# Scaling expert results as they leave PSUM, and accumulating them into x by DMA

## The chip, the cores and the metric

One core of a Trainium2 chip runs the whole program in one launch. The metric is the time of one execution on the device, in microseconds (us). The engines are TensorE (PE, with its weight loads as PEld), VectorE (DVE), ScalarE (ACT), GpSimd (POOL) and SyncE (SP, which only issues DMAs here). POOL issues the indirect DMAs, those whose row numbers come from a tile of indices.

## The reference, cut to what matters

Four steps update x, which has 4 x 512 tokens of 512 numbers. The change touches the second and the seam to the third.

```python
x = x + gat(ctx_512, layernorm(x))           # L0 xattn, two graph attention layers
x = x + moe(layernorm(x))                    # L0 ffn: 8 experts, each token goes to 2
x = x + image_attention(layernorm(x), ctx)   # L1 xattn
x = x + sparse_ffn(layernorm(x))             # L1 ffn, 2:4 sparsity in the hidden layer

# L0 ffn
router_logits = x_flat @ gate_w.T
top_w, sel = top_k(router_logits, 2)
top_w = softmax(top_w)
tw = zeros((n, E)).at[tok_ids, sel].add(top_w)
h  = silu(g) * u                             # g, u: gate and up products of each expert
eo = einsum('enf,edf->end', h, down_proj)
out = einsum('end,ne->nd', eo, tw)           # each token: two expert rows, each by its weight
```

## The kernel before, in words

x lives in SBUF as `X`, 16 tiles of 128 tokens x 512. The program is a row of blocks (`nc.Block`), each with one hand-written instruction stream per engine; semaphores order the streams, and an engine works strictly in the order of its own stream. Every f32 product is three matmuls on a high and a low part (`product3`, lines 72 to 74).

`route` computes, for every token, its two slots among REAL = 39 blocks of 128 slots (`rt["slot"]`, 128 x 32 indices), the two weights (`rt["weight"]`), and the list of tokens of each block. To make that list DVE builds one-hot tiles `blk_hot` (128 x 32 x 39) and `off_hot` (128 x 32 x 128), and PE multiplies them (line 1113).

`moe` runs the 39 blocks of slots. POOL gathers a block's token rows (`m_rows`), PE turns them (line 1402), ACT and DVE split the result, PE forms gate and up, then down into one of two PSUM banks `ACC`; ACT copies that to `y` (`result`, line 1473), and SP stores `y` in the DRAM scratch `y_dram`. The rows stored are not yet scaled.

`image_attention` starts with POOL fetching the rows of y for chunk 0 (4 tiles, 2 rows a token: 8 indirect DMAs into `pair`) and, after the norm of chunk 0, those of chunk 1. Meanwhile the keys are made by PE, ACT and DVE. DVE adds the pairs of chunks 0 and 1, scaled, to X (`add_pairs`, line 1799). For chunks 2 and 3 ACT scales them (`scale_pair`, line 1746) and POOL adds them (`add_pair`, line 1650). Each chunk then goes through: DVE statistics (line 119); POOL 1/sqrt (`pool_rstd_for_act`, lines 132 and 134); ACT normalizes (line 141); PE turns; ACT and DVE split; PE forms o and then the similarities; DVE centres and scales them (lines 1827 to 1846), ACT takes exp (line 1753) and DVE adds to X (line 1851). The norm of chunk b + 1 stands inside the work on chunk b, at i = 0 of the loop over i, and needs chunk b + 1 complete in X. POOL also makes one small number a tile (`rs_of`, line 1659), in line with its DMAs. `ffn` follows.

What sets the order around the change is thus each engine's hand-written stream. The functions are below.

Of the kernel before, what the change touches and what calls it, by code (L numbers as in the profile page):

```python
# [15 lines left out]
BF16 = mybir.dt.bfloat16  # L16
# [970 lines left out]
def route(nc, outer, dram):  # L987
# [8 lines left out]
    with ExitStack() as ctx:  # L996
# [41 lines left out]
        lane_b = sb("lane_b", [P, 1], BF16)  # L1038
        off_hot = sb("off_hot", [P, J, P], BF16)
        blk_hot = sb("blk_hot", [P, J, REAL], BF16)  # L1040
        blk_tok = sb("blk_tok", [P, J, 2, REAL], BF16)
# [222 lines left out]
def moe(nc, outer, dram):  # L1264
# [10 lines left out]
    with ExitStack() as ctx:  # L1275
# [11 lines left out]
        hT_lo = sb("hT_lo", [P, 2, RE, P], F32R)  # L1287
        y = sb("y", [P, 2, D])

        GATE = [ps[:, 0, 0:FE], ps[:, 1, 0:FE]]  # L1290
# [12 lines left out]
        gu_lo, dn_lo = sem("m_gu_lo"), sem("m_dn_lo")  # L1303
        index_ready = sem("m_index_ready")
        gu_hi, dn_hi, ld_gu, ld_dn = rt["gu_hi"], rt["dn_hi"], rt["ld_gu"], rt["ld_dn"]

# [24 lines left out]
        with nc.Block() as block:  # L1331
# [66 lines left out]
            def _(pe):  # L1398
# [31 lines left out]
                def body(g, j, i):  # L1430
# [20 lines left out]
                turn_rows(1, 1)  # L1451
                pipeline(pe, body)
                turn_hidden(REAL - 1, 0)
# [3 lines left out]
            def _(act):  # L1457
# [39 lines left out]
                rows_hi(1, 1)  # L1497
                split(1, slice(1, 2), range(DC))
                pipeline(act, body)
                hidden_hi(REAL - 1, 0)  # L1500
# [6 lines left out]
            def _(dve):  # L1507
# [40 lines left out]
                dve.memset(hid[:, :, :], 0.0).then_inc(hid_made, 2)  # L1548
                dve.wait_ge(hid_made, 2)
                dve.sem_inc(gu_lo, 1)  # L1550
                rows_lo(0, 0)
                hidden(0, 0)
# [11 lines left out]
def image_attention(nc, outer, dram):  # L1564
# [7 lines left out]
    with ExitStack() as ctx:  # L1572
        def sb(name, shape, dt=F32):
            return ctx.enter_context(nc.sbuf_tensor("a_" + name, shape, dt))

        pair = [sb(f"pair{k}", [P, D]) for k in range(2 * TB)]
        x_hi = sb("x_hi", [P, 2, DC, N], F32R)
# [36 lines left out]
        dve_chain = sem("a_dve_chain")  # L1614
        paired = [sem(f"a_paired{k}") for k in range(2 * TB)]
        added, scaled, summed = sem("a_added"), sem("a_scaled"), sem("a_summed")

        with nc.Block() as block:
            @block.sync
            def _(sp):  # L1620
                sp.dma_start(gamma[:, :], dram["gamma"].broadcast_to([P, N])).then_inc(ld_row, 16)
                sp.dma_start(beta[:, :], dram["beta"].broadcast_to([P, N])).then_inc(ld_row, 16)

                sp.wait_ge(added, 4 * TB)
                for r in range(2):
                    sp.dma_start(outer["raw_gu"][:, r, :, :], dram["ffn_gu"][r]).then_inc(outer["ld_gu"][r], 16)
                for r in range(RQ):
                    sp.dma_start(outer["raw_dn"][:, r, :], dram["ffn_dn"][r]).then_inc(outer["ld_dn"][r], 16)

            @block.gpsimd  # L1630
            def _(pool):
                def gather(c, i):

                    for k in range(2):
                        if c in (1, 2):
                            pool.wait_ge(added, TB * (2 * c - 2 + k) + i + 1)
                        if c == 3:
                            pool.wait_ge(summed, 2 * i + k + 1)
                        j = 2 * (TB * c + i) + k
                        pool.indirect_dma_start(out=pair[2 * i + k][:, :], out_offset=None, in_=rt["y_dram"],  # L1640
                                                in_offset=bass.IndirectOffsetOnAxis(ap=rt["slot"][:, j:j + 1], axis=0)
                                                ).then_inc(paired[2 * i + k], 16)

                def add_pair(c, i):
                    t, n = TB * c + i, 2 * (TB * (c - 2) + i)
                    for k in range(2):
                        pool.wait_ge(scaled, n + k + 1)
                        if k == 1:
                            pool.wait_ge(summed, n + 1)
                        pool.tensor_tensor(X[:, t, :], X[:, t, :], pair[2 * i + k][:, :], ALU.add).then_inc(summed, 1)  # L1650

                for i in range(TB):
                    gather(0, i)
                norm.pool_rstd_for_act(pool, 0)
                for i in range(TB):
                    gather(1, i)
                def rs_of(t):
# [70 lines left out]
            def _(act):  # L1728
# [12 lines left out]

                def scale_pair(c, i):
                    for k in range(2):
                        t, pk = TB * c + i, pair[2 * i + k]
                        act.wait_ge(paired[2 * i + k], 16 * (c + 1))
                        act.activation(pk[:, :], pk[:, :], ACT.Identity,
                                       scale=rt["weight"][:, t, k:k + 1]).then_inc(scaled, 1)

                def exp_of(t):
# [19 lines left out]
                for b in range(B):  # L1769
                    for i in range(TB):  # L1770
# [3 lines left out]
                        if b + 1 < B and i % 2 == 0:  # L1774
# [7 lines left out]
                        if b + 2 < B and i >= 1:  # L1782
                            scale_pair(b + 2, i - 1)
                    if b + 1 < B:
                        o_hi_of(b + 1)
                    if b + 2 < B:
                        scale_pair(b + 2, TB - 1)

            @block.vector
            def _(dve):  # L1790
                chain = Chain(dve, dve_chain)
                def add_pairs(c, k):

                    for i in range(TB):
                        t = TB * c + i
                        dve.wait_ge(paired[2 * i + k], 16 * (c + 1))
                        if k == 1:
                            dve.wait_ge(added, 2 * TB * c + i + 1)
                        dve.scalar_tensor_tensor(out=X[:, t, :], in0=pair[2 * i + k][:, :],
                                                 scalar=rt["weight"][:, t, k:k + 1], in1=X[:, t, :],  # L1800
                                                 op0=ALU.mult, op1=ALU.add).then_inc(added, 1)
                    dve.wait_ge(added, TB * (2 * c + k + 1))

                def x_lo_of(c, i):
# [3 lines left out]
                for b in range(B):  # L1808
# [4 lines left out]
                    dve.tensor_scalar(kvT[:, :], KVB, bk[:, 0:1], None, ALU.add).then_inc(kvT_made, 1)  # L1813
                    if b >= 2:
                        add_pairs(0, b - 2)
                    dve.wait_ge(kvT_hi_done, b + 1)
# [31 lines left out]
                def add_prob(t):  # L1848
# [3 lines left out]
                                             in1=X[:, t, :], op0=ALU.mult, op1=ALU.add).then_inc(x_added, 1)  # L1852

                norm.dve_stats_for_act(chain, 0)
                dve.wait_ge(ld_row, 32)
# [5 lines left out]

                add_pairs(1, 0)
# [253 lines left out]
def build(nc, dram, out):  # L2116
    with ExitStack() as ctx:
# [39 lines left out]
        with ExitStack() as kv_inputs, ExitStack() as experts:  # L2157
# [6 lines left out]
            for name, shape in (("gu_w", [P, 2, DC, 2, FE]), ("dn_w", [P, 2, RE, D])):  # L2164
                for part in ("_hi", "_lo"):
                    route_[name + part] = experts.enter_context(nc.sbuf_tensor(name + part, shape, F32R))
            route(nc, outer, dram)
            moe(nc, outer, dram)
# [65 lines left out]
```

## Time and profile before

| | |
|---|---|
| times of three runs | 1205.3, 1206.35, 1206.38 us; median 1206.35 |
| profiled execution | 1207.65 us, of which the span of the profile is 1205.9 |
| busy share | PE 81%, PEld 67%, DVE 56%, ACT 30%, POOL 23% |
| route ends, moe starts | 198.3 us from the span's start |
| moe ends, attention starts | 484.4 us |
| attention's last DVE operation ends | 646.29 us |

A profile row of the timeline gives the start, the duration, the engine, the line in the kernel, the operation, what it writes and reads, and in brackets how long the engine had been idle and which event ended that. For POOL, DMA_INDIRECT is the time in which POOL writes the transfer's descriptors; the data moves afterwards. PEclk is the TensorE clock that was granted: 1.00 is 2.4 GHz, 0.50 is 1.2 GHz.

### The profile page before, as it was taken

Reading aid. Unit: us, or ns where it says so; the run is one execution under the profiler, and the core shown is the slowest. Engines: PE = TensorE matmul, PEld = TensorE weight load, DVE = VectorE, ACT = ScalarE, POOL = GpSimd, SP = SyncE. Lnnn points to the kernel's source line nnn. Section 1 sums busy time; section 2 is a strip of 40 time slices with the busy share of each in tenths; the row PEclk is TensorE's granted clock in tenths of the full one; section 3 lists DMA queues with packets and bytes.
Section 4 is the critical chain, followed back from the end, with each engine's and each line's share of the span. In section 5 each row is a group of like instructions: output and inputs, shape, how many; then the busy total and the mean of one; then the engine's idle time right before and its main releaser. Section 6 shows DMA issues by size and latency. Waiting matters only on the chain. (4 is left out here: it accounts for less than half of the span.)

```text
span 1205.9 us, 15539 instructions
## 1 busy us (share of the span) xinstructions
PE 972.1 (81%) x4555; PEld 806.1 (67%) x4556; DVE 673.8 (56%) x1391; ACT 363.4 (30%) x608; POOL 283.1 (23%) x297
## 2 busy tenths in 40 slices
PE   4980711999999998433356789999999999999996
PEld 3760311899999997222245678888888888888885
DVE  6963775343243522576788754554556555454545
ACT  4760310342243433223333321322132212212220
POOL 0574131223123510446613200301011100301000
PEclk8995765999999999576667989999999999999998
DMA  8165303444244421341201100201001100100001
GB/s 335 45 143 95 131 9 136 146 144 170 70 144 152 161 78 44 105 157 42 63 1 48 58 1 2 70 1 35 0 35 35 35 0 0 35 0 1 35 35 70
DMA packets 35833, 86.32 MB, mean 72 GB/s; under 512 B 5840, under 2 KB 5968, under 8 KB 34512
## 3 DMA queue, kind: packets, MB, share of 16 engines
q1 hardware_dynamic: 27216, 62.76, 14.8%
q0 software_dynamic: 8576, 23.08, 7.2%
q8 instruction: 18, 0.29, 0.1%
q14 instruction: 23, 0.19, 0.1%
HBM read 63.01 MB, written 22.81 MB: 71 GB/s over the span
## 5 line engine op out<-in xcount | busy, mean ns | idle before, releaser
L72 PE MATMUL ps<-f_x_lo,f_w_hi 128*128 128x512 f32 x512 | 202.9, 396 | 14.1 <-POOL f_w_lo L919 7.3
L73 PE MATMUL ps<-f_x_hi,f_w_lo 128*128 128x512 f32 x512 | 201.8, 394 | 0.0
L74 PE MATMUL ps<-f_x_hi,f_w_hi 128*128 128x512 f32 x512 | 201.6, 394 | 0.0
L981 DVE TENSOR_TENSOR f_hid<-f_sg,ps 128x512 f32<-128x512 f32 x64 | 43.7, 684 | 196.7 <-ACT f_sg L976 196.5
L72 PEld LDWEIGHTS ps<-f_x_lo,f_w_hi 128*128 128x128 f32 x512 | 97.6, 191 | 35.8 <-DVE f_hid L981 7.2
L74 PEld LDWEIGHTS ps<-f_x_hi,f_w_hi 128*128 128x128 f32 x512 | 97.7, 191 | 20.7
L73 PEld LDWEIGHTS ps<-f_x_hi,f_w_lo 128*128 128x128 f32 x512 | 97.7, 191 | 20.4
L72 PE MATMUL ps<-gu_w_lo,m_xT_hi 128*128 (+1 forms) x312 | 105.8, 339 | 3.1 <-DVE m_xT_lo L1510 3.1
L976 ACT ACTIVATE f_sg<-ps 128x512 f32<-128x512 f32 x64 | 38.2, 599 | 227.4 <-PE ps L74 227.1
L72 PE MATMUL ps<-f_w_lo,kv_c_hi 128*128 128x512 f32 x256 | 102.1, 399 | 5.4 <-DVE x L2102 5.4
L73 PE MATMUL ps<-f_w_hi,kv_c_lo 128*128 128x512 f32 x256 | 102.0, 398 | 0.0
L74 PE MATMUL ps<-f_w_hi,kv_c_hi 128*128 128x512 f32 x256 | 101.8, 398 | 0.0
L74 PE MATMUL ps<-gu_w_hi,m_xT_hi 128*128 (+1 forms) x312 | 101.4, 325 | 0.0
L73 PE MATMUL ps<-gu_w_hi,m_xT_lo 128*128 (+1 forms) x312 | 101.3, 325 | 0.0
L919 POOL TENSOR_TENSOR f_w_lo<-raw,f_w_hi 128x1024 fp32r<-128x1024 f32 x16 | 38.5, 2406 | 252.9 <-ACT f_w_hi L909 252.9
L1520 DVE TENSOR_TENSOR m_hT_lo<-ps,m_hT_hi 128x384 fp32r<-128x384 f32 x39 | 21.7, 555 | 115.2 <-ACT m_hT_hi L1464 97.2
L2001 ACT CAST kv_c_hi<-f_hid 128x1024 fp32r<-128x1024 f32 x32 | 33.6, 1050 | 149.7 <-PE ps L74 117.7
L2067 DVE TENSOR_TENSOR f_beats<-kv_c_raw 128x768 bf16<-128x768 f32 (+2 forms) x96 | 65.7, 739 | 22.7 <-ACT kv_c_raw L1995 18.8
L159 PE MATMUL ps<-ident,a_a_xn 128*128 128x128 f32 x64 | 15.7, 427 | 65.7 <-ACT a_a_xn L141 64.3
L72 PEld LDWEIGHTS ps<-gu_w_lo,m_xT_hi 128*128 128x128 f32 x312 | 59.2, 190 | 8.9 <-issue 4.9
L72 PEld LDWEIGHTS ps<-f_w_lo,kv_c_hi 128*128 128x128 f32 x256 | 48.6, 190 | 17.3 <-DVE kv_c_lo L2096 5.8
L73 PEld LDWEIGHTS ps<-gu_w_hi,m_xT_lo 128*128 128x128 f32 x312 | 59.3, 190 | 0.5
(301 smaller groups left out, 1930.6 us busy)
## 6 DMA issues: line engine op xcount, KB each, us to landing
raw<-in_moe_gu SPq DMA_DIRECT2D x32, 352.0 KB
y_scratch<-m_y SPq DMA_DIRECT2D x39, 256.0 KB
raw<-in_ffn_gu SPq DMA_DIRECT2D x16, 512.0 KB, 3.5
raw<-in_moe_dn SPq DMA_DIRECT2D x24, 256.0 KB
x<-in_x SPq DMA_DIRECT2D x4, 1024.0 KB, 13.3
gat_rows<-g_ybuf SPq DMA_DIRECT2D x16, 256.0 KB
xn_scratch<-r_r_xn SPq DMA_DIRECT2D x16, 256.0 KB, 2.2
raw<-in_ffn_dn SPq DMA_DIRECT2D x16, 256.0 KB
```

The lines of the kernel that those rows point to most:

```text
L72: eng.matmul(out, lhs_hi, rhs_lo, start=start, stop=False)
L73: eng.matmul(out, lhs_lo, rhs_hi, start=False, stop=False)
L74: return eng.matmul(out, lhs_hi, rhs_hi, start=False, stop=stop)
L159: ins = eng.transpose(bank[:, P * d:P * d + P], self.xn[:, t % self.nb, P * d:P * d + P], self.ident[:, :])
L919: pool.tensor_tensor(self.w_lo[r][:, 0:2, :], self.raw_gu[:, r % self.slots, :, :], self.w_hi[r][:, 0:2, :].bitcast(F32), ALU.subtract).th ...
L976: act.activation(sg[:, k, :], self.GATE[k], ACT.Silu).then_inc(self.silu, 1)
L981: dve.tensor_tensor(out, sg[:, k, :], self.UP[k], ALU.mult).then_inc(self.hid_made, 1)
L1520: dve.tensor_tensor(hT_lo[:, k, :, :], HB.rearrange("p (r n) -> p r n", r=RE), hT_hi[:, k, :, :].bitcast(F32), ALU.subtract).then_inc(h_lo ...
L2001: act.copy(hid_hi[:, 0, :, half], hid[:, :, half]).then_inc(u.hid_hi_done, 1)
L2067: ins = dve.tensor_tensor(beats[:, at:at + n, :], mag[:, i, half].unsqueeze(1).broadcast_to([P, n, HN]), mag[:, j0:j1, half], ALU.is_ge)
```

## The change

Each slot's weight is now brought into slot order. At the start of `moe` DVE writes the weights as a sum of three bf16 terms (five small operations), multiplies `blk_hot` by each term (three operations of 128 x 1248), PE multiplies by `off_hot` in 32 matmuls of 117 columns into `ACC[1]`, and DVE adds the three parts to `slot_weight` (128 x 39). `result` becomes an activation Identity with that scale. For this `off_hot` and `blk_hot` live on after `route`. In `image_attention` the tiles `pair`, `add_pairs`, `scale_pair` and `add_pair` go; POOL fetches the rows with accumulating indirect DMAs straight into X, first all k = 0 of a chunk and then all k = 1, and DVE waits on `second_in` before it takes a chunk's statistics.

```diff
+                pe.wait_ge(weight_hot, 1)
+                for j in range(2 * T):
+                    ins = pe.matmul(ACC[1][:, 0:3 * REAL], off_hot[:, j, :],
+                                    blk_weight[:, j, :, :].rearrange("p w b -> p (w b)"), start=(j == 0),
+                                    stop=(j == 2 * T - 1))
+                ins.then_inc(weight_sum, 1)
                 turn_rows(0, 1)
...
-                    act.copy(y[:, k, :], ACC[k]).then_inc(y_done, 1)
+                    at = slice(g, g + 1) if isinstance(g, int) else bass.ds(g, 1)
+                    act.activation(y[:, k, :], ACC[k], ACT.Identity, scale=slot_weight[:, at]).then_inc(y_done, 1)
...
+                for n in range(3):
+                    ins = dve.tensor_tensor(blk_weight[:, :, n, :], blk_hot[:, :, :],
+                                            weight_b[:, n, :].unsqueeze(2).broadcast_to([P, 2 * T, REAL]), ALU.mult)
+                ins.then_inc(weight_hot, 1)
...
-                sp.wait_ge(added, 4 * TB)
+                sp.wait_ge(second_in[1], 16 * TB)
...
+                def fetch(c, k, tiles):
+
+                    for i in tiles:
+                        t = TB * c + i
                         if k == 1:
+                            pool.wait_ge(first_in[i], 16 * (c + 1))
+                        pool.indirect_dma_start(out=X[:, t, :], out_offset=None, in_=rt["y_dram"],
+                                                in_offset=bass.IndirectOffsetOnAxis(
+                                                    ap=rt["slot"][:, 2 * t + k:2 * t + k + 1], axis=0),
+                                                compute_op=ALU.add).then_inc((first_in[i], second_in[c])[k], 16)
+
+                for k in range(2):
+                    fetch(0, k, range(TB))
+                for k in range(2):
+                    fetch(1, k, range(TB))
                 norm.pool_rstd_for_act(pool, 0)
-                for i in range(TB):
-                    gather(1, i)
...
-                            gather(b + 2, i)
-                            if i >= 1:
-                                add_pair(b + 2, i - 1)
-                    if b + 2 < B:
-                        add_pair(b + 2, TB - 1)
+                            fetch(b + 2, i // 2, range(TB // 2 * (i % 2), TB // 2 * (i % 2) + 2))
...
-                    if b == 0:
-                        add_pairs(1, 1)
-                    else:
-                        dve.wait_ge(summed, 2 * TB * b)
+                    dve.wait_ge(second_in[b + 1], 16 * TB)
```

POOL's stream at the start of the attention block, before: line 1640 is a fetch, lines 132 and 134 are the norm, 1659 is `rs_of`, 1650 an addition to x.

```order
L1640 DMA a_pair<-y_scratch,slot 128x512 x8
L132 TENSOR_TENSOR a_a_rstd<-a_a_var_eps,minus_half 128x4
L134 TENSOR_TENSOR a_a_minus_mean<-a_a_minus_mean,a_a_rstd 128x4
L1640 DMA a_pair<-y_scratch,slot 128x512 x8
L1659 TENSOR_TENSOR a_rs<-a_ve,minus_half 128x1 x2
L132 TENSOR_TENSOR a_a_rstd<-a_a_var_eps,minus_half 128x4
L134 TENSOR_TENSOR a_a_minus_mean<-a_a_minus_mean,a_a_rstd 128x4
L1640 DMA a_pair<-y_scratch,slot 128x512 x2
```

The same place in the changed kernel, where line 1680 is the accumulating fetch and 1692 is `rs_of`:

```order
L1680 DMA x<-y_scratch,slot 128x512 x16
L132 TENSOR_TENSOR a_a_rstd<-a_a_var_eps,minus_half 128x4
L134 TENSOR_TENSOR a_a_minus_mean<-a_a_minus_mean,a_a_rstd 128x4
L1692 TENSOR_TENSOR a_rs<-a_ve,minus_half 128x1 x2
L132 TENSOR_TENSOR a_a_rstd<-a_a_var_eps,minus_half 128x4
L134 TENSOR_TENSOR a_a_minus_mean<-a_a_minus_mean,a_a_rstd 128x4
L1680 DMA x<-y_scratch,slot 128x512 x2
```

The eight fetches of chunk 1 stood behind the first norm and now stand ahead of it.

DVE's stream at the start of `moe`, in the changed kernel; before, line 1525's operation came straight behind the memset:

```order
L1563 MEMSET m_hid 128x768
L1566 CAST m_weight_b<-weight 128x32
L1568 TENSOR_TENSOR m_weight_rest<-weight,m_weight_b 128x32
L1570 CAST m_weight_b<-m_weight_rest 128x32
L1572 TENSOR_TENSOR m_weight_rest<-m_weight_rest,m_weight_b 128x32
L1574 CAST m_weight_b<-m_weight_rest 128x32
L1577 TENSOR_TENSOR m_blk_weight<-blk_hot,m_weight_b 128x32x39 x3
L1584 COPY m_slot_weight<-ps 128x39
L1586 TENSOR_TENSOR m_slot_weight<-m_slot_weight,ps 128x39
L1589 TENSOR_TENSOR m_slot_weight<-m_slot_weight,ps 128x39
L1525 TENSOR_TENSOR m_xT_lo<-ps,m_xT_hi 128x512
```

Eleven small or middle-sized operations have come in between the memset and the split of the first rows; PE's 32 matmuls wait for the first nine of them.

## Rows read from the trace of the kernel before

**Rows 1.** Windows: the ffn, then three stretches within moe.

```profile
core 0: us, PE busy (x) PEld busy (x) DVE busy (x) ACT busy (x) POOL busy (x), PEclk, DMA share, GB/s
637.20:1205.90 568.70, 543.20 (x2352) 443.14 (x2352) 319.44 (x700) 136.20 (x178) 61.60 (x35) 0.98 0.08 26
208.63:211.73 3.10, 3.10 (x10) 3.10 (x11) 0.00 (x0) 0.53 (x1) 0.00 (x0) 0.50 1.02 402
211.96:213.72 1.76, 1.76 (x12) 1.76 (x12) 0.00 (x0) 0.47 (x1) 0.00 (x0) 1.00 0.07 28
216.30:474.00 257.70, 257.67 (x1519) 238.06 (x1519) 94.18 (x148) 93.52 (x178) 73.56 (x115) 1.00 0.37 126
```

**Rows 2.** Timeline of DVE and PE, end of route and start of moe.

```profile
183.34 0.18 DVE L1224 TENSOR_SCALAR r_at<-slot 128x32 int32<-128x32 int32 x1
186.74 1.45 DVE L1233 TENSOR_TENSOR r_blk_tok<-r_blk_hot,r_lane_b 128x1248 bf16<-128x1248 bf16 x1
192.58 2.26 PE L1113 MATMUL ps<-r_blk_tok,r_off_hot 128*128 128x78 bf16 x32 [17.64 <-DVE r_off_hot L1235]
198.74 0.70 DVE L1548 MEMSET m_hid<- 128x768 f32 x1 [0.79 <-DVEq L1055]
206.12 1.11 PE L1402 MATMUL ps<-ident,m_rows 128*128 128x128 f32 x4 [11.27 <-DMA m_rows<-xn_scratch,m_index]
```

**Rows 3.** Groups of ACT, whole span.

```profile
L1473 ACT COPY m_y<-ps 128x512 f32<-128x512 f32 x39 | 22.9, 587 | 54.1 <-PE ps L74 51.0 <-issue 3.0
L1746 ACT ACTIVATE a_pair<-a_pair,weight 128x512 f32<-128x512 f32 x16 | 11.1, 715 | 16.2 <-DMA a_pair<-y_scratch,slot 16.2
```

**Rows 4.** Timeline of POOL, start of the attention.

```profile
485.14 0.94 POOL L1640 DMA_INDIRECT a_pair<-y_scratch,slot  x1 [37.98 <-POOLq L1331]
487.64 1.43 POOL L1640 DMA_INDIRECT a_pair<-y_scratch,slot  x1 [0.30 <-issue]
506.62 1.05 POOL L132 TENSOR_TENSOR a_a_rstd<-a_a_var_eps,minus_half 128x4 f32<-128x4 f32 x1 [11.12 <-DVE a_a_var_eps L126]
```

**Rows 5.** Tiles: issue (ns, min/median/max) of accumulating fetches; landing of plain ones (a_pair).

```profile
L337 POOL DMA_INDIRECT x<-gat_rows,g_arg x16: 1539/1548/1597, 63.3 to 103.7; - x16
DMA to landing us min/median/max: 3.4/3.5/3.9
```

**Rows 6.** Timeline and windows, plain and accumulating fetches of the first stage.

```profile
74.61 0.94 POOL L315 DMA_INDIRECT g_arg<-gat_arg,g_place  x1 [0.31 <-issue]
103.67 1.55 POOL L337 DMA_INDIRECT x<-gat_rows,g_arg  x1 [0.30 <-issue]
...
107.00:109.00 2.00, 0.00 (x0) 0.00 (x0) 0.00 (x0) 0.00 (x0) 0.00 (x0) 0.50 0.59 101
109.00:110.00 1.00, 0.00 (x0) 0.00 (x0) 0.00 (x0) 0.00 (x0) 0.00 (x0) 0.50 0.03 4
```

**Rows 7.** Timeline of DVE in the attention.

```profile
487.56 0.69 DVE L1817 TENSOR_TENSOR a_kvT_lo<-a_kvT,a_kvT_hi 128x512 fp32r<-128x512 f32 x1 [0.69 <-ACT a_kvT_hi L1731]
503.39 2.46 DVE L119 BATCH_NORM_STATS2 a_a_stats<-x 128x6 f32<-128x512 f32 x4
527.43 2.73 DVE L1799 SCALAR_TENSOR_TENSOR x<-a_pair,weight,x 128x512 f32<-128x512 f32 x4
540.59 1.44 DVE L1843 SCALAR_TENSOR_TENSOR kv_c_raw<-kv_c_raw,a_rs,a_beta 128x512 f32<-128x512 f32 x1
575.76 1.51 DVE L1843 SCALAR_TENSOR_TENSOR kv_c_raw<-kv_c_raw,a_rs,a_beta 128x512 f32<-128x512 f32 x1
613.07 0.74 DVE L1843 SCALAR_TENSOR_TENSOR kv_c_raw<-kv_c_raw,a_rs,a_beta 128x512 f32<-128x512 f32 x1
```

**Rows 8.** Timeline of POOL and DVE, chunk 2 becoming complete.

```profile
556.80 0.55 POOL L1659 TENSOR_TENSOR a_rs<-a_ve,minus_half 128x1 f32<-128x1 f32 x1 [5.62 <-DVE a_ve L1830]
558.84 0.95 POOL L1640 DMA_INDIRECT a_pair<-y_scratch,slot  x1 [0.30 <-issue]
565.43 2.47 DVE L119 BATCH_NORM_STATS2 a_a_stats<-x 128x6 f32<-128x512 f32 x4 [3.78 <-POOL x L1650]
```

More of the change, by code:

```diff
@@ L1288, in moe @@
         y = sb("y", [P, 2, D])
+        off_hot, blk_hot = rt["off_hot"], rt["blk_hot"]
+        weight_b = sb("weight_b", [P, 3, 2 * T], BF16)
+        rest = sb("weight_rest", [P, 2 * T])
+        blk_weight = sb("blk_weight", [P, 2 * T, 3, REAL], BF16)
+        slot_weight = sb("slot_weight", [P, REAL])
         GATE = [ps[:, 0, 0:FE], ps[:, 1, 0:FE]]
@@ L1304, in moe @@
         index_ready = sem("m_index_ready")
+        terms, weight_hot, weight_sum, weight_made = (
+            sem("m_" + n) for n in ("terms", "weight_hot", "weight_sum", "weight_made"))
         gu_hi, dn_hi, ld_gu, ld_dn = rt["gu_hi"], rt["dn_hi"], rt["ld_gu"], rt["ld_dn"]
@@ L1451, in _ @@
                 turn_rows(1, 1)
+                pe.wait_ge(weight_made, 2)
                 pipeline(pe, body)
@@ L1498, in _ @@
                 split(1, slice(1, 2), range(DC))
+                act.wait_ge(weight_made, 2)
                 pipeline(act, body)
@@ L1549, in _, with slot_weights @@
                 dve.wait_ge(hid_made, 2)
+                weights = rt["weight"][:, :, :].rearrange("p t k -> p (t k)")
+                dve.tensor_copy(weight_b[:, 0, :], weights).then_inc(terms, 1)
+                dve.wait_ge(terms, 1)
+                dve.tensor_tensor(rest[:, :], weights, weight_b[:, 0, :], ALU.subtract).then_inc(terms, 1)
+                dve.wait_ge(terms, 2)
+                dve.tensor_copy(weight_b[:, 1, :], rest[:, :]).then_inc(terms, 1)
+                dve.wait_ge(terms, 3)
+                dve.tensor_tensor(rest[:, :], rest[:, :], weight_b[:, 1, :], ALU.subtract).then_inc(terms, 1)
+                dve.wait_ge(terms, 4)
+                dve.tensor_copy(weight_b[:, 2, :], rest[:, :]).then_inc(terms, 1)
+                dve.wait_ge(terms, 5)
+                for n in range(3):
+                    ins = dve.tensor_tensor(blk_weight[:, :, n, :], blk_hot[:, :, :],
+                                            weight_b[:, n, :].unsqueeze(2).broadcast_to([P, 2 * T, REAL]), ALU.mult)
+                ins.then_inc(weight_hot, 1)
+                def slot_weights():
+                    dve.wait_ge(weight_sum, 1)
+                    sums = ACC[1]
+                    dve.tensor_copy(slot_weight[:, :], sums[:, 0:REAL]).then_inc(weight_made, 1)
+                    dve.wait_ge(weight_made, 1)
+                    dve.tensor_tensor(slot_weight[:, :], slot_weight[:, :], sums[:, REAL:2 * REAL],
+                                      ALU.add).then_inc(terms, 1)
+                    dve.wait_ge(terms, 6)
+                    dve.tensor_tensor(slot_weight[:, :], slot_weight[:, :], sums[:, 2 * REAL:3 * REAL],
+                                      ALU.add).then_inc(weight_made, 1)
                 dve.sem_inc(gu_lo, 1)
+                slot_weights()
                 rows_lo(0, 0)
@@ L1574, in sb @@
             return ctx.enter_context(nc.sbuf_tensor("a_" + name, shape, dt))
-        pair = [sb(f"pair{k}", [P, D]) for k in range(2 * TB)]
         x_hi = sb("x_hi", [P, 2, DC, N], F32R)
@@ L1614, in image_attention @@
         dve_chain = sem("a_dve_chain")
-        paired = [sem(f"a_paired{k}") for k in range(2 * TB)]
-        added, scaled, summed = sem("a_added"), sem("a_scaled"), sem("a_summed")
+        first_in = [sem(f"a_first_in{i}") for i in range(TB)]
+        second_in = [sem(f"a_second_in{c}") for c in range(B)]
         with nc.Block() as block:
@@ L1631, in _ @@
             def _(pool):
[L1632 to L1647, printed above, removed]
-                        if k == 1:
-                            pool.wait_ge(summed, n + 1)
-                        pool.tensor_tensor(X[:, t, :], X[:, t, :], pair[2 * i + k][:, :], ALU.add).then_inc(summed, 1)
-                for i in range(TB):
-                    gather(0, i)
+                def fetch(c, k, tiles):
+                    for i in tiles:
+                        t = TB * c + i
+                        if k == 1:
+                            pool.wait_ge(first_in[i], 16 * (c + 1))
[7 more added lines that the diff above has]
+                    fetch(1, k, range(TB))
                 norm.pool_rstd_for_act(pool, 0)
-                for i in range(TB):
-                    gather(1, i)
                 def rs_of(t):
@@ L1740, in x_hi_of @@
                     norm.act_hi(act, TB * c + i, x_hi[:, c % 2, :, P * i:P * i + P])
[L1742 to L1747, printed above, removed]
                 def exp_of(t):
@@ L1791, in _ @@
                 chain = Chain(dve, dve_chain)
[L1792 to L1802, printed above, removed]
                 def x_lo_of(c, i):
@@ L1852, in add_prob @@
                                              in1=X[:, t, :], op0=ALU.mult, op1=ALU.add).then_inc(x_added, 1)
+                dve.wait_ge(second_in[0], 16 * TB)
                 norm.dve_stats_for_act(chain, 0)
@@ L2166, in build @@
                     route_[name + part] = experts.enter_context(nc.sbuf_tensor(name + part, shape, F32R))
+            route_.update({
+                "off_hot": experts.enter_context(nc.sbuf_tensor("off_hot", [P, 2 * T, P], BF16)),
+                "blk_hot": experts.enter_context(nc.sbuf_tensor("blk_hot", [P, 2 * T, REAL], BF16)),
+            })
             route(nc, outer, dram)
```

10 lines of the change are left out of this document (1 added, 9 removed).

## The prediction

> **What bounds the kernel now.** I read the windows first. In moe from 216.3 on and in the ffn PE is never idle for long: 257.67 of 257.70 us, and 543.20 of 568.70 [rows 1]. So what delays the start of either stage is not made up in it, and what ACT, DVE or POOL do inside moe costs nothing while it fits behind PE. ACT is busy 93.5 of those 257.7 us. The change can act at three places: the start of moe, the end of moe, and the attention, where no engine is the bound. There the timeline shows a chain that goes from engine to engine: statistics on DVE, 1/sqrt on POOL, normalizing on ACT, turning on PE, splitting, products, centring on DVE. Each wait is to be read by what arrives last.
>
> At the start of moe PE waits 11.27 us for the first gathered rows and turns them at 206.12 [rows 2]. At the start of the attention POOL issues eight fetches from 485.14 on; DVE's statistics of chunk 0 start at 503.39 [rows 7], and POOL's 1/sqrt follows at 506.62 after 11.12 us of idleness, released by DVE [rows 4]. POOL has slack there, DVE none. Chunks 2 and 3 are different: the statistics at 565.43 waited 3.78 us for POOL's additions [rows 8].
>
> **Start of moe.** DVE is free at 198.74 + 0.70 = 199.44. Five operations on 128 x 32, at 0.18 each as the nearest row plus some 0.03 between dependent ones, are 1.05: 200.5. Three products of 128 x 1248 in bf16 at 1.45 less the usual small overlap, 4.2 in all: 204.7 [rows 2]. Then PE: 32 matmuls of 78 columns took 2.26 us at the same low clock; by columns, 117 of them give 2.26 x 1.5 = 3.4, and if the columns don't set the pace, 2.3. I take 3.3: 208.0. The rows landed by 206.12, so turning them comes 1.9 us later. The three small additions that follow on DVE (0.6) run while PE turns (1.11) and ACT splits; they cost nothing, and would cost up to 0.6 if that cover were gone. **+1.9**, bounds +0.9 and +2.6. The clock can shift this: the first products ran at 1.2 GHz for 10 matmuls in 3.10 us, then 12 in 1.76 [rows 1]. PE will have been busy for over 3 us before it turns the rows, so the clock may already be up; that gives back at most 10 x (0.31 - 0.147) = 1.6. If all 24 products ran at the low clock it would cost 14 x 0.163 = 2.3 more. I count nothing and keep both for the range.
>
> **Scaling at the evacuation.** 39 copies of 587 ns become activations with a scale tile. The nearest row, an activation with such a scale from SBUF, took 715 [rows 3]: at most 0.13 each, 5 us of ACT's time behind PE, free but for the last, whose store ends the block: **+0.1**. The waits on `weight_made` are met long before.
>
> **First norm of the attention.** An accumulating fetch costs POOL 1548 ns of issue (1539 to 1597 over 16) [rows 5] against 0.94 us for a plain one, and 0.30 lie between two [rows 4]. The changed stream has 16 of them ahead of the first 1/sqrt, where 8 plain ones stood. The last issue ends at 485.14 + 15 x 1.85 + 1.55 = 514.4, and 1/sqrt starts some 0.2 later: 514.6 instead of 506.62, +8.0 (these times leave out the 2.0 by which moe shifts everything). DVE's statistics don't delay it: chunk 0's last fetch starts at 498.1 and lands within 5.3 (below), at 503.4, as now, so they end near 506.5 and then 8 us of waiting follow on POOL. This is the wait that takes the place of the DVE additions; behind it on POOL's queue stand `rs_of` and all later norms, so ACT, PE and DVE all wait. Fetches can be stretched: the one at 487.64 took 1.43 while DVE ran an operation on two SBUF tiles [rows 4, 7], and four such operations remain. I add 0.2, bounds 0 and 1.5. **+8.2**.
>
> The Trainium skill, SBUF — State Buffer, Who interferes with whom, says that `tensor_tensor` takes only the read side of the port pair that DVE and GpSimd share, and infers that writing descriptors needs the other, so such a fetch shouldn't be stretched. This trace disagrees for that one fetch (1.43 against 0.95). By the rule the sum would be 0.2 lower.
>
> **What DVE no longer does.** The eight additions for chunk 0 and the first four for chunk 1 lay on time that the wait on POOL now covers or that ACT covered: nothing. The last four for chunk 1 stood right ahead of the statistics of chunk 1: 2.73 us [rows 7], on the path: **-2.7**. Chunk 1 will be in X by then (last fetch starts at 512.9; DVE asks near 535).
>
> **What POOL no longer does.** The scaling of y at 540.59 took 1.44 and that at 575.76 took 1.51, both while POOL was adding pairs; without such neighbours it took 0.74 at 613.07 [rows 7]. ACT's exp and the second half of the norm wait for it. **-0.7 and -0.8**. ACT's 16 scalings (11.1 us [rows 3]) lay in its own waiting time: nothing.
>
> **Chunks 2 and 3.** Now: `rs_of` at 556.80, the second fetch at 558.84, additions, statistics at 565.43, 8.63 after `rs_of` [rows 8]. Then: two accumulating fetches follow `rs_of`, the second starting at +0.74 + 1.85 = +2.6, and the statistics wait for its landing. How long a landing takes is not shown directly. A plain one takes 3.5 from the start of its issue, so 2.5 from the end of it [rows 5]: lower end 1.55 + 2.5 = 4.05. In the first stage the last accumulating fetch started at 103.67, and DMA work went on until 109.0 [rows 6], behind a backlog: upper end 5.3. I take 4.9, nearer the row of the same kind. The statistics then start at +7.5, 1.1 earlier than now (bounds 0.7 and 2.0), twice: **-2.2**. `rs_of` for later tiles moves behind 3.4 us of issue instead of 2.3, with over 1 us to spare.
>
> The Trainium skill, DMA: Bandwidth & Descriptors, Anatomy of one DMA, gives some 2.0 us plus bytes / 436e3 from software-made descriptors, 2.6 for 256 KB. It fits the plain fetch (2.5). Taken for the accumulating one as well, as an estimate, the landing would be 4.15 and the sum 1.5 lower.
>
> **Sum**: 1.9 + 0.1 + 8.2 - 2.7 - 0.7 - 0.8 - 2.2 = +3.8. The profiled execution took 1207.65 and would take 1211.4; it stands 1.3 above the median of 1206.35, and the sum on that gives **1210.1 us**.
>
> **Rivals.** A measurement of this kernel tells some 0.2% (2.4 us) from no change.
> *Given back* (within 0.2%): the clock is up when moe's products start (-1.6), or the landings are short (-1.8). Either brings the sum near 2. For it speaks that PE works right up to those products; against it, that after an earlier idle stretch ten matmuls went by before the clock rose. Time 1208.1.
> *Issue at the plain rate* (faster): the 1.55 belongs to the first stage and not to accumulating. Then 16 fetches need 15 x 1.25 + 0.95, until 504.8, the first norm is not delayed, and the terms are 2.0 - 6.4 = -4.4, and about 2 less again if chunk 0 lands sooner: 1202. The point from which it decides: the sum is zero if the first 1/sqrt starts 8.2 - 3.8 = 4.4 late, 25.9 after the first fetch (now 21.5). Against it: a plain fetch in the same stage, some 29 us before the last accumulating one, took 0.94 [rows 6], so accumulating is what costs.
> *Queue behind itself* (slower still): the DMA engines can't follow. Work went on 3.8 us after the last issue in the first stage [rows 6]. If a k = 1 fetch must wait on its k = 0 one, or the fetches are stretched as much as the worst (0.5 each over 16), 8 us come on top of the 8.2, and the time is 1218 at the most, 1215 if half.
> *The change does what it says but the weights are late*: DVE's products take twice as long beside POOL's gathers, +4.2 more: 1214.
>
> **How the numbers follow.** My forecast, slower by 1.5 to 7: 0.62, of which a part of 0.04 lies within 0.2%. Given back: 0.2. Plain rate, or another saving I price too low: 0.09. The two slower rivals: 0.09 together. So faster 0.09, same 0.24, slower 0.67. The likeliest case's own range is 1208 to 1213.5: the sum with its bounds -1.0, -1.8 and the clock below, and +0.7, +1.3, +0.8 and a part of the clock's 2.3 above. With the neighbours, 1206.3 to 1213.8.
>
> **What would show it.** Step by step in the changed profile: 32 matmuls of 117 columns from about 204.7 to 208.0, rows turned then; the ACTIVATE of m_y below 720 ns and no gap of PE in moe; accumulating fetches 1.85 apart, 16 of them, from the attention's start; the first 1/sqrt 29.7 after the first fetch, released by no engine; statistics of chunk 1 straight behind the first row maximum; the two long scalings back at 0.74; the statistics of chunks 2 and 3 about 7.5 after `rs_of`, released by a DMA. Wrong it would be if the 1/sqrt comes at once behind the statistics, if landings are much longer than 5.3, or if activations from PSUM with a scale tile make PE wait for `y_done`.

## The result, and the profile after

The changed kernel took 1210.61 us (median of 11 runs), the kernel before 1206.38 (11 runs, the three shown above among them): a ratio of 1.0034, 95% interval 1.0020 to 1.0048. It is slower by 4.2 us where 3.8 were forecast, and inside the range. Its profiled execution took 1211.32, with a span of 1209.6.

**Start of moe.** Timeline of all engines in the changed kernel, the lines that matter:

```profile
198.86 0.70 DVE L1563 MEMSET m_hid<- 128x768 f32 x1 [0.79 <-DVEq L1054]
199.22 1.08 POOL L1376 DMA_INDIRECT m_rows<-xn_scratch,m_index  x1 [0.30 <-issue]
...
200.80 4.20 DVE L1577 TENSOR_TENSOR m_blk_weight<-blk_hot,m_weight_b 128x1248 bf16<-128x1248 bf16 x3
200.97 2.17 POOL L1376 DMA_INDIRECT m_rows<-xn_scratch,m_index  x1 [0.15 <-issue]
...
205.06 3.33 PE L1455 MATMUL ps<-m_blk_weight,off_hot 128*128 128x117 bf16 x32 [10.08 <-DVE m_blk_weight L1577]
...
208.18 0.91 PE L1408 MATMUL ps<-ident,m_rows 128*128 128x128 f32 x4
...
210.49 0.43 PE L72 MATMUL ps<-gu_w_lo,m_xT_hi 128*128 128x352 f32 x1 [1.40 <-DVE m_xT_lo L1525]
```

The three products took 4.20 as priced, the matmuls 3.33 (priced 3.3), and the rows are turned at 208.18, 2.1 later than at 206.12 [rows 2]. PE's matmuls waited for eight of the eleven new DVE operations (five small ones and the three products), not for nine. But the first of the gate and up products takes 0.43 and those behind it are issued 0.16 apart: the granted clock is 1.00 from 210.50 to 214.40, where ten matmuls ran at 1.2 GHz before [rows 1]. The turning and the products now come behind 32 weight matmuls, at which PE had worked for 3.33 us. The second tile of rows is turned here in the changed kernel:

```profile
214.43 0.60 PE L1408 MATMUL ps<-ident,m_rows 128*128 128x128 f32 x4
```

and here in the kernel before:

```profile
214.05 0.60 PE L1402 MATMUL ps<-ident,m_rows 128*128 128x128 f32 x4
```

Counted from each kernel's memset that is 15.57 and 15.31. Of 1.9 us only 0.3 is left there in this execution.

**Evacuation.** Group of ACT in the changed kernel (mean ns behind the busy time):

```profile
L1487 ACT ACTIVATE m_y<-ps,m_slot_weight 128x512 f32<-128x512 f32 x39 | 26.9, 689 | 57.6 <-PE ps L74 52.7 <-issue 4.9
```

It is 0.10 each above the copy's 587 [rows 3], hidden behind PE but for the last: from the end of PE's last product of moe to the attention's first fetch it is 7.33 us, before 7.22.

**First norm of the attention.** Timeline of POOL in the changed kernel, its 16 fetches shown by the first two and the last:

```profile
485.06 1.58 POOL L1680 DMA_INDIRECT x<-y_scratch,slot  x1 [38.14 <-POOLq L1337]
486.94 1.56 POOL L1680 DMA_INDIRECT x<-y_scratch,slot  x1 [0.30 <-issue]
...
513.09 1.56 POOL L1680 DMA_INDIRECT x<-y_scratch,slot  x1 [0.30 <-issue]
514.07 1.66 POOL L132 TENSOR_TENSOR a_a_rstd<-a_a_var_eps,minus_half 128x4 f32<-128x4 f32 x1
```

And DVE's statistics (line 119) of the same kernel, with the first half of what the second chunk does:

```profile
504.28 2.47 DVE L119 BATCH_NORM_STATS2 a_a_stats<-x 128x6 f32<-128x512 f32 x4 [5.25 <-DMA x<-y_scratch,slot]
536.32 2.46 DVE L119 BATCH_NORM_STATS2 a_a_stats<-x 128x6 f32<-128x512 f32 x4
546.71 0.74 DVE L1847 SCALAR_TENSOR_TENSOR kv_c_raw<-kv_c_raw,a_rs,a_beta 128x512 f32<-128x512 f32 x1
569.23 2.48 DVE L119 BATCH_NORM_STATS2 a_a_stats<-x 128x6 f32<-128x512 f32 x4 [3.22 <-DMA x<-y_scratch,slot]
602.72 2.47 DVE L119 BATCH_NORM_STATS2 a_a_stats<-x 128x6 f32<-128x512 f32 x4 [3.29 <-DMA x<-y_scratch,slot]
```

POOL's 1/sqrt has no bracket: no engine released it, POOL was never idle. DVE's numbers for it were there at 507.44, but it ends at 515.73, before at 506.62 + 1.05 = 507.67 [rows 4]. The statistics of chunk 1 come straight behind other work, those of chunks 2 and 3 wait for a landing. DVE's waits in the attention, changed kernel (in all, times, longest):

```profile
DVE a_x_lo L168 <- ACT a_x_hi L164: 21.8, 11, 11.4
DVE a_a_stats L119 <- DMA x<-y_scratch,slot: 11.8, 3, 5.3
```

and the kernel before:

```profile
DVE a_x_lo L168 <- ACT a_x_hi L164: 14.4, 11, 4.2
DVE a_a_stats L119 <- POOL x L1650: 7.6, 2, 3.8
```

The longest wait for ACT's split grew by 7.2: the delayed norm, seen by an engine that stands further down the chain. DVE has 4.8 us less to do in the span (669.0 against 673.8 busy) and ACT 5.9 less; neither was the bound.

The following table gives each event's time since POOL's first fetch (485.14 before, 485.06 after).

| event | before | after | difference |
|---|---|---|---|
| first 1/sqrt ends | 22.53 | 30.67 | +8.1 |
| first chunk's o is split (DVE) | 35.82 | 44.79 | +9.0 |
| statistics of chunk 1 start | 45.05 | 51.26 | +6.2 |
| statistics of chunk 2 start | 80.29 | 84.17 | +3.9 |
| statistics of chunk 3 start | 115.07 | 117.66 | +2.6 |
| ffn's first DVE operation (line 149) | 161.65 | 164.75 | +3.1 |

### The profile page after: what moved, and what is told of

Read it like the earlier page. It is cut to its first block and busy times, and to the rows that moved or that the text cites. A ratio compares the mean times of both kernels' runs of the same rounds, so it can differ in the third digit from the quotient of the medians.

```text
span 1209.6 us, 15583 instructions
## 1 busy us (share of the span) xinstructions
PE 974.0 (81%) x4587; PEld 808.1 (67%) x4588; DVE 669.0 (55%) x1386; ACT 357.5 (30%) x592; POOL 281.8 (23%) x281
## 3 DMA queue, kind: packets, MB, share of 16 engines
q1 hardware_dynamic: 27216, 62.76, 14.9%
## 5 line engine op out<-in xcount | busy, mean ns | idle before, releaser
L73 PEld LDWEIGHTS ps<-f_x_hi,f_w_lo 128*128 128x128 f32 x512 | 97.8, 191 | 20.4
L159 PEld LDWEIGHTS ps<-ident,a_a_xn 128*128 128x128 f32 x64 | 12.6, 223 | 75.3 <-ACT a_a_xn L141 55.7
L1680 POOL DMA_INDIRECT x<-y_scratch,slot x32 | 51.4, 1605 | 46.5 <-POOLq L1337 38.1
```

What stands on the lines that cost most here:

```text
L73: eng.matmul(out, lhs_lo, rhs_hi, start=False, stop=False)
L159: ins = eng.transpose(bank[:, P * d:P * d + P], self.xn[:, t % self.nb, P * d:P * d + P], self.ident[:, :])
L1680: pool.indirect_dma_start(out=X[:, t, :], out_offset=None, in_=rt["y_dram"], in_offset=bass.IndirectOffsetOnAxis(ap=rt["slot"][:, 2 * t + ...
```

## The experiments

Theory A is the prediction's: the order on POOL's queue decides. The 16 issues of 1.55 us ahead of the first 1/sqrt cost 8, and the fetches that stand behind `rs_of` make the statistics of chunks 2 and 3 late. Each expectation names its rivals. For the readings I use the attention's length, from POOL's first fetch to the first line 149 of ffn: it leaves out that the profiled executions reach moe up to 3.4 us apart (memset between 196.31 and 199.69). Each ratio is to executions of the kernel before that were timed beside it: their median is 1206.38 beside the changed kernel, 1207.37 beside e1 to e4, 1207.06 beside e5 to e8 and 1207.55 beside e9. So a difference between two medians of the table can be off by about 1 us.

| kernel | median us | ratio to before | 95% | attention |
|---|---|---|---|---|
| before | 1206.4 to 1207.6 | 1 | | 161.65 |
| after | 1210.61 | 1.0034 | 1.0020 to 1.0048 | 164.75 |
| e1 norm ahead of chunk 1's fetches | 1202.44 | 0.9965 | 0.9954 to 0.9977 | 157.64 |
| e2 last fetches ahead of `rs_of` | 1203.90 | 0.9980 | 0.9969 to 0.9991 | 157.84 |
| e3 both | 1196.41 | 0.9909 | 0.9896 to 0.9922 | 150.57 |
| e4 attention's part alone | 1209.77 | 1.0021 | 1.0010 to 1.0031 | 164.76 |
| e5 moe's part alone | 1208.89 | 1.0018 | 1.0008 to 1.0028 | 161.95 |
| e6 plain fetches into x | 1197.38 | 0.9920 | 0.9906 to 0.9933 | 150.92 |
| e7 before, PE warmed | 1204.78 | 0.9980 | 0.9968 to 0.9993 | 161.23 |
| e8 before, fetch, scaling and adding early | 1206.84 | 0.9998 | 0.9989 to 1.0007 | 162.81 |
| e9 before, fetch alone early | 1203.53 | 0.9962 | 0.9949 to 0.9976 | 157.82 |

**e1_norm_first.** Is it the order, or the fetches themselves, that delays the norm?

```diff
                 for k in range(2):
                     fetch(0, k, range(TB))
+                norm.pool_rstd_for_act(pool, 0)
                 for k in range(2):
                     fetch(1, k, range(TB))
-                norm.pool_rstd_for_act(pool, 0)
```

> The changed kernel with POOL's 1/sqrt of chunk 0 ahead of chunk 1's eight fetches, nothing else. Theory A (the first norm pays for standing behind those fetches): 1/sqrt starts about 22.4 us after the first fetch, when the statistics end, instead of 29.0; all that follows comes some 7 us earlier; time about 1203.5 us, 2.8 below the kernel before. Rival B (the DMA engines are the bound, the wait only moves on): the statistics of chunk 1 then wait for the landing of its last fetch, the gain is 4 us or less, and the time 1206.5 or more.

Timeline of POOL in e1:

```profile
506.11 1.05 POOL L132 TENSOR_TENSOR a_a_rstd<-a_a_var_eps,minus_half 128x4 f32<-128x4 f32 x1 [7.33 <-DVE a_a_var_eps L126]
507.60 1.62 POOL L1680 DMA_INDIRECT x<-y_scratch,slot  x1 [0.16 <-issue]
```

POOL again waits for DVE, 22.05 after its first fetch, and the kernel is 8.2 us faster than the changed one (7.1 in the attention). The eight fetches behind the norm cost nothing there: chunk 1's statistics start without a bracket, 8.6 sooner than in the changed kernel. Of these 1.3 are lost again before the statistics of chunk 2. The order is the cause of the first term.

**e2_early_last.** The second half of k = 1 goes ahead of `rs_of` (and ahead of the 1/sqrt of ffn that stands there).

```diff
+                        if b + 2 < B and i == TB - 1:
+                            fetch(b + 2, 1, range(TB // 2, TB))
                         if i == TB - 1 and b in (1, 2):
                             fnorm.pool_rstd(pool, b - 1)
                         if TB * b + i + 1 < T:
                             rs_of(TB * b + i + 1)
...
-                        if b + 2 < B:
+                        if b + 2 < B and i < TB - 1:
                             fetch(b + 2, i // 2, range(TB // 2 * (i % 2), TB // 2 * (i % 2) + 2))
```

> The changed kernel with the last two fetches of chunks 2 and 3 moved ahead of the small 1/sqrt at i = 3, which waits for the centring of the next chunk. Theory A: the statistics of chunks 2 and 3 lose their waits of 3.2 and 3.3 us, time 6.5 us below the changed kernel, about 1204. Rival B (DMA-bound): landings stretch and 3 us or less is gained.

Timeline of POOL in e2:

```profile
551.69 1.57 POOL L1680 DMA_INDIRECT x<-y_scratch,slot  x1 [0.30 <-issue]
553.56 1.56 POOL L1680 DMA_INDIRECT x<-y_scratch,slot  x1 [0.30 <-issue]
559.53 0.56 POOL L1692 TENSOR_TENSOR a_rs<-a_ve,minus_half 128x1 f32<-128x1 f32 x1 [4.40 <-DVE a_ve L1836]
```

and of DVE, chunks 2 and 3:

```profile
563.92 2.46 DVE L119 BATCH_NORM_STATS2 a_a_stats<-x 128x6 f32<-128x512 f32 x4
593.98 2.46 DVE L119 BATCH_NORM_STATS2 a_a_stats<-x 128x6 f32<-128x512 f32 x4
```

No brackets any more: the 3.22 and 3.29 us of waiting are gone, and 6.7 us of time with them (6.9 in the attention). POOL has room for both fetches, since it is idle 4.40 us before `rs_of` even so.

**e3_both.** Do the two places add, or does one hide the other?

> Both moves together. Theory A: the two gains add, 13.5 us below the changed kernel, about 1197 us, 9 below the kernel before. Rival B: chunk 1's fetches and chunk 2's come closer together and the sum is 8 us or less.

They add: 8.2 and 6.7 make 14.9, measured 14.2, and the same 14.2 in the attention's length. None of the statistics of chunks 1 to 3 waits (527.26, 557.54 and 587.84, without brackets). This kernel is 0.9% faster than before.

**e4_attention_alone** and **e5_moe_alone** divide the change. e4 takes the attention of the changed kernel and everything else of before, so it leaves out the weights of the expert rows; e5 is the reverse, with the attention's weights replaced by 1:

```diff
-                                                 scalar=rt["weight"][:, t, k:k + 1], in1=X[:, t, :],
+                                                 scalar=1.0, in1=X[:, t, :],
...
-                                       scale=rt["weight"][:, t, k:k + 1])
+                                       scale=1.0)
```

> Only the attention's part of the change: accumulating fetches in the changed order, with moe as before, so the expert rows are added without their weights. Theory A: the attention's start to end is 3 us longer than before and all of the loss is there, time about 1209.5 with moe's start costing nothing measurable. Rival C (the loss is moe's start, which the forecast priced at 1.9): this kernel is only 1.5 to 2 above the kernel before, 1208.

> Only moe's part of the change: slot weights and the scaled evacuation; the attention fetches, multiplies by 1 and adds as before, with the same instructions, so the result is the reference's. Theory A: a little under the 1.9 of the forecast, since the clock is up sooner: 0.5 to 2 above the kernel before. Rival D (moe's part is free, all is given back by the clock): no difference. Rival E (the scale tile makes the evacuation slow or late): 4 or more above.

1.0021 x 1.0018 = 1.0039, beside 1.0034 for the whole. By the times each part costs 1.8 to 2.5 us, so that e4's Theory A, which put all of the loss in the attention, holds for the profiles but not for the times. e4's attention is as long as the changed kernel's (164.76 and 164.75), e5's 0.3 longer than before's. From memset to the attention's first fetch moe takes 286.1 to 286.6 in the six profiles with the weights, and 286.4, 285.8 and 286.0 in those of before, e4 and e9. In e8, which has before's moe as well, it took 288.3: there nineteen of the first matmuls passed at the low clock, where it was ten in before, and PE turned the second tile of rows 17.3 after the memset instead of 15. So one and the same moe differs by 2 us between executions with the moment at which the clock rises. On average the profiles with the weights are 0.2 above the three (0.3 below, if e8 is counted), the times about 2 (1.0 to 3.4). e5's profiled execution was the fastest of its nine (1206.8). Where the rest comes in, in executions that left no trace, stays open.

**e6_plain_into_x.** What does accumulating cost by itself? The order stays, and `compute_op` goes, so that each fetch writes over the tile of x and the output leaves out what was there.

```diff
-                                                    ap=rt["slot"][:, 2 * t + k:2 * t + k + 1], axis=0),
-                                                compute_op=ALU.add).then_inc((first_in[i], second_in[c])[k], 16)
+                                                    ap=rt["slot"][:, 2 * t + k:2 * t + k + 1], axis=0)).then_inc((first_in[i], second_in[c])[k], 16)
```

> The changed kernel with the same fetches in the same order, but without the addition: each writes its rows over the tile of x, so the output leaves out what x held. Theory A (accumulating costs issue time, 1.55 against 0.95, and landing time): the first 1/sqrt starts about 20 us after the first fetch instead of 29, the statistics of chunks 2 and 3 come 2 us sooner each, time 1197 to 1199. Rival F (the order alone is at fault, whatever a fetch costs): the 1/sqrt still comes more than 25 us after the first fetch and the time stays above 1205.

The fetches as the view of the tile `y_scratch` shows them (issue in ns, min/median/max; then the landing in us, from the start of the issue), in e6:

```profile
L1680 POOL DMA_INDIRECT x<-y_scratch,slot x32: 942/950/1432, 484.8 to 584.7; - x32
DMA to landing us min/median/max: 3.4/3.6/3.8
```

and in the changed kernel:

```profile
L1680 POOL DMA_INDIRECT x<-y_scratch,slot x32: 1544/1567/1901, 485.1 to 597.6; - x32
DMA to landing us min/median/max: 4.7/5.3/6.0
```

With the same lines of code and the same rows, accumulating costs 0.6 of issue and 1.7 of landing a fetch, and in this order 13.2 us of the kernel's time; the first 1/sqrt comes 20.4 after the first fetch. e3, which accumulates, is as fast as e6: a better order gives as much as cheaper fetches would in the order of the change. This also puts down the rival "issue at the plain rate".

**e7_warm_clock.** The kernel before, with 24 matmuls of the identity ahead of its first turning, to see what the clock is worth there.

```diff
+                for j in range(24):
+                    pe.matmul(ACC[1][:, 0:P], ident[:, :], ident[:, :], start=True, stop=True)
                 turn_rows(0, 1)
```

> The kernel before with 24 idle products of the identity into an unused bank while PE waits for moe's first rows. Theory A (PE's work just ahead of moe's first products lifts their clock): the first 24 products of gate and up take some 4 us instead of 5.3, time 1 to 1.6 below the kernel before. Rival: no difference, since the clock falls again in the 1.4 us before the products or since the rows' landing sets the start.

Timeline of PE in e7:

```profile
204.68 0.60 PE L1402 MATMUL ps<-ident,m_rows 128*128 128x128 f32 x4
206.68 0.43 PE L72 MATMUL ps<-gu_w_lo,m_xT_hi 128*128 128x352 f32 x1 [1.40 <-DVE m_xT_lo L1512]
206.94 0.32 PE L73 MATMUL ps<-gu_w_hi,m_xT_lo 128*128 128x352 f32 x1
```

The products run at 2.4 GHz from the first. It gained 2.3 us (interval 0.8 to 3.9) where 1 to 1.6 were expected; 0.5 of it is that the turning is shorter as well (0.60 against 1.11 [rows 2]). The 32 weight matmuls give back time in the same way in the changed kernel. It is a saving of its own, which the kernel before can have without the change.

**e8_before_early** and **e9_gather_early.** Would before gain by the same reordering? e8 moves fetch, scaling and addition of the last tile of chunks 2 and 3 forward: POOL's ahead of `rs_of`, ACT's ahead of its cast of o (`o_hi_of`).

```diff
+                        if i == TB - 1 and b + 2 < B:
+                            gather(b + 2, i)
+                            add_pair(b + 2, i - 1)
+                            add_pair(b + 2, i)
...
+                    if b + 2 < B:
+                        scale_pair(b + 2, TB - 1)
                     if b + 1 < B:
                         o_hi_of(b + 1)
-                    if b + 2 < B:
-                        scale_pair(b + 2, TB - 1)
```

> The kernel before with the last fetch, scalings and additions of chunks 2 and 3 moved ahead of the small 1/sqrt at i = 3. Theory A (POOL's order, not the way of adding, makes the statistics of chunks 2 and 3 wait): both waits of 3.8 us go, time 7 us below the kernel before, about 1200; accumulating by DMA in the best order (e3) is then worth some 3 us more. Rival G: the additions make the small 1/sqrt late instead, and 3 us or less is gained.

It gained nothing, though both waits of 3.8 us are gone: the statistics of chunks 2 and 3 start without a bracket. The attention is even 1.2 longer, in a profiled execution that was the slowest of its eleven (1211.94). Timeline of ACT in e8:

```profile
558.24 0.72 ACT L1748 ACTIVATE a_pair<-a_pair,weight 128x512 f32<-128x512 f32 x1 [3.59 <-DMA a_pair<-y_scratch,slot]
559.71 0.72 ACT L1748 ACTIVATE a_pair<-a_pair,weight 128x512 f32<-128x512 f32 x1 [0.75 <-DMA a_pair<-y_scratch,slot]
560.34 0.56 ACT L1768 CAST a_o_hi<-ps 128x512 fp32r<-128x512 f32 x1
```

and DVE's waits there:

```profile
DVE a_o_lo L1862 <- ACT a_o_hi L1768: 13.0, 3, 7.4
```

where the kernel before has

```profile
DVE a_o_lo L1860 <- ACT a_o_hi L1766: 5.0, 3, 3.8
```

The cast of o stands behind two scalings that wait for a landing, and DVE waits 13.0 us for it instead of 5.0. The wait was moved, not removed. The time is that of *Rival G*, but not its reason: `rs_of` at 564.55 found POOL idle for 2.12 us, so the additions didn't make it late. e9 moves POOL's fetch alone, and no scaling or addition:

```diff
+                        if i == TB - 1 and b + 2 < B:
+                            gather(b + 2, i)
                         if i == TB - 1 and b in (1, 2):
                             fnorm.pool_rstd(pool, b - 1)
...
                         if b + 2 < B:
-                            gather(b + 2, i)
+                            if i < TB - 1:
+                                gather(b + 2, i)
```

> The kernel before, with only POOL's last two fetches of chunks 2 and 3 moved ahead of the 1/sqrt that they stood behind (POOL had been idle 5.62 us there at 556.80, and 1.93 and 2.21 us at 588.34 and 591.58); scalings and additions keep their places, so nothing stands ahead of ACT's cast of o. Theory A (in the old scheme too the late fetch is what the statistics of chunks 2 and 3 wait for, and the last such experiment failed only by what it moved ahead of ACT's cast): the rows land near 556.0, ACT scales them before POOL has finished its 1/sqrt at 557.35, four additions end at 562.9, so the statistics start at 563.0 instead of 565.43, and 2.3 earlier in chunk 3 as well: 4.7 in all, median 1202.3. Rival G (the wait for those rows has no slack behind it either, something else on ACT or POOL comes late at once): within 1 us of before, 1206.5 to 1207.5, with the statistics of chunk 2 still near 565.

DVE's statistics of chunks 2 and 3 in e9:

```profile
562.99 2.47 DVE L119 BATCH_NORM_STATS2 a_a_stats<-x 128x6 f32<-128x512 f32 x4 [1.15 <-POOL x L1650]
595.22 2.47 DVE L119 BATCH_NORM_STATS2 a_a_stats<-x 128x6 f32<-128x512 f32 x4 [1.15 <-POOL x L1650]
```

The attention is 3.8 us shorter (4.7 expected), and the kernel 4.0. What is left, 1.15 twice, are POOL's additions behind `rs_of`, which accumulating does away with. So the late fetch was a cost of before, too, and a fairer comparison of the two schemes is that of the best orders tried here, e3 with e9: 150.57 against 157.82 in the attention, ratios of 0.9909 and 0.9962 to before (five executions each).

## Why the prediction was right

**First norm, +8.2.** Right in mechanism and size: 16 issues 1.87 apart, 1/sqrt released by nothing, its end 8.1 later; e1 took the delay away and with it 8.2 us. One step was less exact: the last fetch of chunk 0 took 6.0 from the start of its issue (498.24) to the statistics (504.28), not at most 5.3, and these start 0.9 later than before. POOL's queue hid that; in e1, where it doesn't, 1/sqrt starts 22.05 after the first fetch instead of 21.5.

**DVE's additions, -2.7.** The table of events falls from +9.0 to +6.2 between the split of o and the statistics of chunk 1: 2.8. The 0.9 by which it had risen before that is a term that I didn't have. It is PE's product for o, 12 matmuls. Timeline of PE, first and last of them, in the changed kernel:

```profile
523.70 0.79 PE L72 MATMUL ps<-a_x_lo,a_kv_hi 128*128 128x512 f32 x1 [1.40 <-DVE a_x_lo L168]
...
528.56 0.63 PE L74 MATMUL ps<-a_x_hi,a_kv_hi 128*128 128x512 f32 x1
```

and in the kernel before:

```profile
515.64 0.79 PE L72 MATMUL ps<-a_x_lo,a_kv_hi 128*128 128x512 f32 x1 [1.40 <-DVE a_x_lo L168]
...
519.84 0.40 PE L74 MATMUL ps<-a_x_hi,a_kv_hi 128*128 128x512 f32 x1
```

A matmul of 0.63 is one at 1.2 GHz, one of 0.40 at 2.4 GHz. In the changed kernel PE went through all twelve at the low level (5.49 us, granted clock 0.50), where before the last four ran at the high one (4.60 us, 0.63 on average): 0.9. That the longer wait for the norm is the reason isn't shown: e6, whose norm came sooner than before's (20.4 after the first fetch), went through all twelve at the low level too, and e8, with before's norm, through eleven.

**POOL beside DVE, -0.7 and -0.8.** The scaling at 546.71 takes 0.74, as does its counterpart in chunk 2; they took 1.44 and 1.51 [rows 7].

**Chunks 2 and 3, -2.2.** Timeline of POOL in the changed kernel, `rs_of` and the last fetch of chunk 2:

```profile
561.51 0.56 POOL L1692 TENSOR_TENSOR a_rs<-a_ve,minus_half 128x1 f32<-128x1 f32 x1 [8.20 <-DVE a_ve L1834]
564.16 1.69 POOL L1680 DMA_INDIRECT x<-y_scratch,slot  x1 [0.30 <-issue]
```

The statistics start at 569.23: 7.72 after `rs_of`, against 8.63 [rows 8] before and 7.5 forecast. So each gave 0.9 where I had 1.1. They start 5.07 after the last fetch; I had taken 4.9, between bounds of 4.05 and 5.3.

The Trainium skill, DMA: Bandwidth & Descriptors, Anatomy of one DMA, would have given 4.15 by the way in which the prediction used it, an estimate that sets its 2.6 behind the end of the issue. Read so, the plain fetches of e6 agree with it (3.6 from the issue's start, of which 0.95 is issue); the accumulating ones (4.7 to 6.0) don't. But the Trainium skill counts setup and descriptor writing into its fixed 2.0 on that page, and then its 2.6 for the whole is too low for the plain ones as well.

**Attention in sum.** Forecast 8.2 - 2.7 - 1.5 - 2.2 = +1.8, measured +3.1. The clock, for which the sum had no term here, makes some +1.2: besides the 0.9 above, chunk 1's product for o is 0.7 shorter than before, chunk 2's 0.3 longer, and the first similarity product of the last chunk 0.7 longer, each time by how many of its matmuls met the low level. The landings add 0.4, and -0.3 is left in small differences. The close total thus owes something to luck: these clock terms could have come out otherwise. **Start of moe, +1.9** was off the other way in the profile. Its delay was sized rightly (2.1), but the rival *given back* was true of the clock, and the sum counted nothing for it: 0.3 stayed, and moe as a whole was as long as before (286.2 and 286.4). ffn took 559.8 instead of 559.1 from its first line 149 to the end, for which I had no term; over the eleven profiles, with the same ffn, it took 558.9 to 560.1, and its cause wasn't sought. The misses nearly cancel, so that the total of the profiled execution (+3.7 for +3.8) looks better than its terms. By the times, moe's part is nearer to what I took (1.0 to 3.4), and that difference between profiles and times is left open. So the forecast time is borne out, and the attention's mechanisms with it; for moe's 1.9 it isn't shown that the time arises where the forecast put it.

**The rivals.** *Given back* happened to the moe term alone, and the landings weren't short. *Issue at the plain rate* is put down by the 1.55 in this stage and by e6, *queue behind itself* by the 16 steady issues, and the late weights by 4.20 us for the three products, though a gather beside them was stretched.

## What to carry to other kernels

Moving work from an engine into a DMA moves its cost to the queue that issues it. Here DVE and ACT were spared 11 us of busy time, of which only DVE's last four additions for chunk 1 (2.7) stood on the path, and POOL got three times the issue time (25 us instead of 8) in front of a tiny 1/sqrt that all others waited for. When fetches get dearer, go through that queue again: put each small result that others wait for ahead of every issue that isn't needed yet, and each last fetch into idle time in front of it; here that was worth 14 us and turned 0.3% slower into 0.9% faster. When moving something forward, look at what stands behind it on every engine that it passes (e8 against e9).

## What was unexpected of the hardware

- POOL's issue can be stretched beside a DVE operation that reads two SBUF tiles. The gather at 200.97 took 2.17 beside the bf16 products, where an undisturbed one takes 1.00, and an accumulating fetch at 542.93 took 1.89 instead of 1.55. What sets the long ones apart is which of the two began first. Of the 64 fetches in the attention, before and after, nine began while such an operation was already running: they took 1.11 to 1.43 (plain) and 1.69 to 1.90 (accumulating). All others took at most 1.03 and 1.63, also where such an operation began during them, as one at 490.72 did in the changed kernel (1.54). That is why, of the four such operations beside the first sixteen fetches, only one cost anything (0.16), and my 0.2 fitted. The Trainium skill, SBUF — State Buffer, Who interferes with whom, infers that `tensor_tensor` leaves descriptor writing alone; the 2.17 here and the 1.43 in [rows 4] disagree.
- A landing of an accumulating fetch of 128 x 512 takes 4.7 to 6.0 us, of a plain one 3.4 to 3.8, and 16 in a row keep the DMA engines busy: the share was 0.87 from 484 to 516 us in the changed kernel. Still they kept pace with an issue every 1.87 us: no landing took more than 6.0.
